# A small conditioning network on TensorE: outputs in four column tiles, transposed back by VectorE

## What is computed

```python
# layer 0, per batch row b; _layer_norm normalizes over the whole 512 x 512 of a row
h = _noise_encoding(t, 128)              # (16, 128), sin and cos
h = silu(h @ W1 + b1)                    # (16, 512)
h = h @ W2 + b2                          # (16, 512)
scale, shift = h @ Wsc + bsc, h @ Wsh + bsh   # (16, 512) each
out = silu(scale * _layer_norm(x, gamma, beta) + shift)
out = out @ W_in + b_in
out = silu(scale * _layer_norm(out, gamma, beta) + shift)
x = out @ W_out + b_out + x
# layer 1, expert e = itok[b]
h = gelu(x @ Wi[e] + bi[e])              # (512, 2048)
r = h @ Wo[e] + bo[e] + x
y = (r - mean) * rsqrt(var + 1e-12) * gamma[e] + beta[e]   # per row of 512
```

## Time and profile before

| | |
|---|---|
| median of three runs | 1784.67 us |
| the profiled execution | 1784.62 us, of which the span of the trace is 1782.8 us |
| TensorE matmuls busy | 1767.7 us, 99% of the span |
| TensorE weight loads busy | 1463.0 us, 82% |
| VectorE busy | 1285.2 us, 72% |
| ScalarE busy | 981.5 us, 55% |
| GpSimd busy | 101.5 us, 6% |
| mean granted TensorE clock | 0.998 of full speed |

### The profile page before, as it was taken

How to read it: one execution, slowest core, us unless ns; L and a number is a source line. 1 busy time by engine, 2 the same in 40 slices (tenths; PEclk the granted TensorE clock), 3 DMA queues, 4 the chain that set the end, 5 groups by cost and what they waited for, 6 DMA issues and landing times.

```text
span 1782.8 us, 22059 instructions
## 1 busy us (share of the span) xinstructions
PE 1767.7 (99%) x7834; PEld 1463.0 (82%) x7834; DVE 1285.2 (72%) x2132; ACT 981.5 (55%) x1562; POOL 101.5 (6%) x197
## 2 busy tenths in 40 slices
PE   9999999999999999999999999999999999999997
PEld 7788888888888888888888888888888888888886
DVE  6956777777677677767777677677777767777565
ACT  6656455565545656456564555555556554565442
POOL 0000000000000000000000000000000000000001
PEclk9999999999999999999999999999999999999999
DMA  7132331423333233332333313333242233322221
GB/s 290 61 124 75 121 110 62 139 101 98 109 100 128 74 118 108 103 110 71 122 109 101 117 61 127 119 107 110 67 142 94 98 110 114 114 74 98 107 95 59
DMA packets 45614, 189.33 MB, mean 106 GB/s; under 512 B 7042, under 2 KB 7042, under 8 KB 29122
## 3 DMA queue, kind: packets, MB, share of 16 engines
q1 hardware_dynamic: 43106, 183.96, 29.2%
q0 software_dynamic: 2400, 3.97, 2.1%
HBM read 171.10 MB, written 16.81 MB: 105 GB/s over the span
## 4 chain that ended last, share of the span: by engine, by line
PE 97%; DVE 1%; issue 0%; DMA 0%; ACT 0%; DVEq 0%; SPq 0%; ACTq 0%
PE out_acc L431 39%; PE hid_ps L431 39%; PE blk_ps L431 18%; DMA x<-in_xT 0%; DVE bn L693 0%; PE blk_ps L375 0%; PE hid_ps L375 0%; PE blk_ps L384 0%; DVE bn_r L812 0%; DVE r_sb L807 0%; ACT work L593 0%; DVE x L761 0%; ACT h_hi L528 0%; DVE x_lo L679 0%; DVE work L748 0%
## 5 line engine op out<-in xcount | busy, mean ns | idle before, releaser
L431 PE MATMUL hid_ps<-x_hi,wi_hi 128*128 128x512 f32 x1024 | 398.7, 389 | 0.5 <-DVE x_lo L679 0.5
L431 PE MATMUL hid_ps<-x_hi,wi_lo 128*128 128x512 f32 x1024 | 398.4, 389 | 0.0
L431 PE MATMUL hid_ps<-x_lo,wi_hi 128*128 128x512 f32 x1024 | 398.4, 389 | 0.0
L431 PE MATMUL out_acc<-wo_hi,g_hi 128*128 128x512 f32 x1024 | 398.3, 389 | 0.0
L431 PE MATMUL out_acc<-wo_lo,g_hi 128*128 128x512 f32 x1024 | 398.3, 389 | 0.0
L431 PE MATMUL out_acc<-wo_hi,g_lo 128*128 128x512 f32 x1024 | 398.3, 389 | 0.0
L581 ACT ACTIVATE g_sb<-hid_ps,bi_sb 128x512 f32<-128x512 f32 x256 | 175.9, 687 | 319.5 <-PE hid_ps L431 319.2
L679 DVE TENSOR_TENSOR g_lo<-g_sb,g_hi 128x512 fp32r<-128x512 f32 x256 | 175.2, 684 | 203.1 <-ACT g_hi L585 201.3
L528 ACT ACTIVATE wo_hi<-stage 128x512 fp32r<-128x512 f32 x256 | 162.0, 633 | 175.9 <-PE out_acc L431 175.9
L679 DVE TENSOR_TENSOR wo_lo<-stage,wo_hi 128x512 fp32r<-128x512 f32 x256 | 176.2, 689 | 71.8 <-ACT wo_hi L528 68.3
L431 PEld LDWEIGHTS hid_ps<-x_hi,wi_hi 128*128 128x128 f32 x1024 | 192.3, 188 | 41.9 <-DVE x_lo L679 1.7
(11 more groups left out here) (91 smaller groups left out, 1664.2 us busy)
## 6 DMA issues: line engine op xcount, KB each, us to landing
stage<-in_expert_w SPq DMA_DIRECT2D x128, 1024.0 KB, 4.8
x<-in_xT SPq DMA_DIRECT2D x15, 1024.0 KB, 7.2
out_y<-r_sb SPq DMA_DIRECT2D x15, 1024.0 KB, 5.2
rows<-in_expert_rows SPq DMA_DIRECT2D x16, 512.0 KB, 6.7
mv_all<-mv_dram POOLq DMA_DIRECT2D x30, 128.0 KB, 4.0
stage<-in_cond_w SPq DMA_DIRECT2D x4, 512.0 KB, 8.7
affine_sb<-in_affine SPq DMA_DIRECT2D x4, 512.0 KB, 11.1
stage<-in_W SPq DMA_DIRECT2D x1, 1024.0 KB, 5.9
```

Of the source, the lines that this page charges most:

```text
L431: last = pe.matmul(dst, w[wp], xs[xp], start=start and i == 0, stop=stop and i == 2)
```

## The change

W2 and the scale/shift weights become the moving operand, the activations the stationary one, 32 columns wide (16 batch rows and 16 zeros). The output has 32 rows of batch then, and each of four groups of output features is written to its own 32 partitions of one bank, so that each matmul uses one column tile of 32 columns. A layer (`layer`) is 16 matmuls of 128 moving columns: 4 chunks of the contraction by 4 column tiles. The host orders the columns of W2, Wsc and Wsh so that a transpose in blocks of 32 x 32 by VectorE brings the features back to the partitions. VectorE does this and adds the bias; ScalarE's evacuations of L544 go. Scale and shift come in two halves of one layer each (chunks 0 and 1, chunks 2 and 3), each with a load of 1024 KB, in place of four parts. The new order of loads is layer 0, half 0, layer 1, half 1, layer 2, layer 3. VectorE's order for the first product is written out anew. Paddings: 7 for 9 and 4 for 5 before the W2 layer, and new ones of 4, 1, 5 and 8.

```diff
-            load_whole(w2_raw, W2, ld_w2)
+            load_turned(w2_raw, W2, ld_w2)
             for c in range(DC):
                 sp.dma_start(x_sb[0][:, c, :], xT[0, c * P:(c + 1) * P, :]).then_inc(ld_first[c], 16)
-            load_cond(0)
             load_layer(0)
-            load_cond(1)
-            load_cond(2)
+            load_turned(cond_raw[0], cond_w[0], ld_cond[0])
             load_layer(1)
-            load_cond(3)
+            load_turned(cond_raw[1], cond_w[1], ld_cond[1])
             load_layer(2)
             load_layer(3)
...
                     if p:
-                        sp.wait_ge(s_mmcond, 2 * p)
+                        sp.wait_ge(s_mmcond, p)
                     else:
-                        sp.wait_ge(s_mm2, 2)
+                        sp.wait_ge(s_mm2, 1)
...
-            def group(bank, n, w, src):
+            def layer(bank, src, w):
                 for c in range(DC):
-                    last = pe.matmul(bank[:, n * WIDE:(n + 1) * WIDE], w[:, c, :], src[:, c, :],
-                                     start=(c == 0), stop=(c == DC - 1))
+                    for j in range(P // BLOCK):
+                        last = pe.matmul(bank[BLOCK * j:BLOCK * (j + 1), 0:P], src[:, c, :], w[:, c, j, :],
+                                         start=(c == 0), stop=(c == DC - 1))
                 return last
...
-            keep_warm(hid_ps[0], 9)
+            keep_warm(hid_ps[0], 7)
...
-            keep_warm(hid_ps[0], 5)
+            keep_warm(hid_ps[0], 4)
             pe.wait_ge(s_pad, 1)
             pe.wait_ge(ld_w2, 16)
             pe.wait_ge(s_m1, DC)
-            for m in range(DC):
-                last = group(blk_ps[1 - m // 2], m % 2, w2_raw[:, :, m * P:(m + 1) * P], m1)
...
+            layer(blk_ps[1], m1, w2_raw).then_inc(s_mm2, 1)
+            keep_warm(blk_ps[0], 4)
+            pe.wait_ge(s_average, 1)
+            pe.wait_ge(s_mv, 1)
+            average_of(0, 0, mv[:, 0, 0:1])
+            keep_warm(blk_ps[0], 1)
             pe.wait_ge(s_sq, 1)
             average_of(0, 1, dev[:, 0, 1:2])
...
+            keep_warm(blk_ps[0], 5)
+
+            def scale_shift(h):
+                pe.wait_ge(ld_cond[h], 16)
+                layer(hid_ps[h], m2, cond_raw[h]).then_inc(s_mmcond, 1)
+
+            pe.wait_ge(s_m2, 1)
+            scale_shift(0)
+            keep_warm(blk_ps[0], 8)
...
             first_block(0, 0, [(m, 0) for m in range(DC)])
-            scale_of(DC - 1)
-            shift_of(DC - 1)
+            scale_shift(1)
             first_block(0, 0, [(m, c) for c in range(1, DC) for m in range(DC)])
...
                 if turn_of(b, which) == 0:
-                    act.wait_ge(s_cond, 2 * (c + 1))
+                    act.wait_ge(s_cond, 2 * (c // (DC // HALVES) + 1))
...
             for c in range(DC):
                 w_hi_part(0, c)
-                scale_shift(c)
                 norm_end(0, 0, [c])
...
+            def cond_out(h):
+                dve.wait_ge(s_mmcond, h + 1)
+                dve.transpose(cond_turned[:, h].rearrange("p k c n -> p (k c n)"), hid_ps[h][:, 0:P]) \
+                   .then_inc(s_condturn, 1)
+                dve.wait_ge(s_condturn, h + 1)
...
+                for k in range(2):
+                    dve.tensor_tensor(cond_sb[:, k, half, :], cond_turned[:, h, k, :, 0:B],
+                                      bias[:, k].unsqueeze(2).to_broadcast([P, DC // HALVES, B]), ALU.add) \
+                       .then_inc(s_cond, 1)
+
+            dve.wait_ge(s_mm2, 1)
+            dve.transpose(m_turned[:, :, :].rearrange("p c n -> p (c n)"), blk_ps[1][:, 0:P]) \
+               .then_inc(s_mturn, 1)
+            dve.wait_ge(s_mturn, 1)
+            dve.tensor_tensor(m2[:, :, :], m_turned[:, :, :],
+                              small_sb[:, B2:B2 + DC].unsqueeze(2).to_broadcast([P, DC, BLOCK]), ALU.add) \
+               .then_inc(s_m2, 1)
             for m in range(DC):
                 stats(0, 0, m)
             first_mean(0)
             centre(0, 0, 0)
             first_var(0)
...
+            affine(0, 0, 0)
+            w_lo_part(0, 0)
+            cond_out(0)
+            centre(0, 0, 1)
+            h_lo_part(0, 0, 0)
+            affine(0, 0, 1)
+            w_lo_part(0, 1)
+            h_lo_part(0, 0, 1)
+            centre(0, 0, 2)
+            affine(0, 0, 2)
+            cond_out(1)
+            w_lo_part(0, 2)
+            centre(0, 0, 3)
+            h_lo_part(0, 0, 2)
+            affine(0, 0, 3)
+            w_lo_part(0, 3)
+            h_lo_part(0, 0, 3)
...
             pool.memset(m1[:, :, B:], 0.0).then_inc(s_pad, 1)
-            pool.memset(m2[:, :, B:], 0.0).then_inc(s_pad, 1)
```

More of the change, by code:

```diff
@@ L158, in build @@
         enc_sin = sb("enc_sin", [P, B])
[L159 to L162, removed]
+        m1 = sb("m1", [P, DC, BLOCK])
+        m2 = sb("m2", [P, DC, BLOCK])
+        m_turned = sb("m_turned", [P, DC, BLOCK])
+        cond_turned = sb("cond_turned", [P, HALVES, 2, DC // HALVES, BLOCK])
+        cond_sb = sb("cond_sb", [P, 2, DC, B])
         bn = sb("bn", [P, DC, 6])
@@ L182, in build @@
         t_sb, cc, small_sb = head_sb[:, 0:B], head_sb[:, B:B + 3], head_sb[:, B + 3:]
-        w2_raw = stage[:, 0].rearrange("p a b n -> p (a b) n")
-        def cond_raw(m):
-            return stage[:, 1 + m // 2, m % 2].rearrange("p k (c n) -> p k c n", n=P)
+        w2_raw, *cond_raw = (stage[:, n].rearrange("p a b (j n) -> p (a b) j n", n=P)
+                             for n in range(1 + HALVES))
         w_raw = [r_sb, x2_turned]
@@ L196, in build @@
         ld_head, ld_idx, ld_w1, ld_w2 = (sem(f"ld_{n}") for n in ("head", "idx", "w1", "w2"))
-        ld_cond = [sem(f"ld_cond{m}") for m in range(DC)]
+        ld_cond = [sem(f"ld_cond{h}") for h in range(HALVES)]
         ld_first = [sem(f"ld_first{c}") for c in range(DC)]
@@ L280, in load_whole, with load_turned @@
                 sp.dma_start(dst[:, :, :], src.rearrange(chunked, p=P)).then_inc(done, 16)
-            def load_cond(m):
-                sp.dma_start(cond_raw(m), cond_w[m].rearrange("p (k c n) -> p k c n", k=2, n=P)) \
-                  .then_inc(ld_cond[m], 16)
+            def load_turned(dst, src, done):
+                sp.dma_start(dst.rearrange("p c j n -> p (c j n)"), src).then_inc(done, 16)
             def load_layer(c):
@@ L541, in _ @@
                                bias=small_sb[:, B1 + m:B1 + m + 1]).then_inc(s_m1, 1)
[L543 to L551, removed]
-                act.wait_ge(s_mmcond, m + 1)
-                cond_part(scale_sb[:, m, :], cond_bank[m], 0, BSC + m).then_inc(s_cond, 1)
-                cond_part(shift_sb[:, m, :], cond_bank[m], 1, BSH + m).then_inc(s_cond, 1)
             def w_hi_part(n, c):
@@ L862, in _ @@
             first_var(0)
-            for c in range(DC):
-                affine(0, 0, c)
-                w_lo_part(0, c)
-                if c + 1 < DC:
-                    centre(0, 0, c + 1)
-                h_lo_part(0, 0, c)
+            affine(0, 0, 0)
[15 more added lines that the diff above has]
+            h_lo_part(0, 0, 3)
             w_lo_part(1, 0)
@@ L1042 @@
                                axis=1),
-        "W1": A["W1"], "W2": A["W2"],
-        "cond_w": np.stack([A["Wsc"], A["Wsh"]]).reshape(2, DC, P, DC, P).transpose(3, 2, 0, 1, 4)
-                    .reshape(DC, P, 2 * DC * P),
+        "W1": A["W1"],
+        "W2": A["W2"].reshape(DC, P, DC, P // BLOCK, BLOCK).transpose(1, 0, 3, 2, 4).reshape(P, DC * D),
+        "cond_w": np.stack([A["Wsc"], A["Wsh"]])
+                    .reshape(2, DC, P, HALVES, DC // HALVES, P // BLOCK, BLOCK)
+                    .transpose(3, 2, 1, 5, 0, 4, 6).reshape(HALVES, P, DC * D),
         "affine": np.stack([A["gamma"].T, A["beta"].T]).reshape(2, DC, P, S).transpose(1, 2, 0, 3)
```

26 lines of the change are left out of this document (6 added, 20 removed).

## The result

The changed kernel takes 1788.59 us in the median of 22 runs (1786.02 to 1789.0), the kernel before 1784.84 us in 22 runs beside it (1784.42 to 1785.94). The ratio is 1.0016, 95% interval 1.001 to 1.0022. So the change is slower, by about as much as the 0.2% that parts "within" from "slower" in the forecast; the forecast itself was slower by 0.7. The time lies in the range. The profiled execution took 1788.71 us, 4.09 more than that of before; its span is 1786.9 us, 4.1 more.

The account below looks back on a forecast made before the run. TensorE, busy throughout from 100 to 1760 us, was taken to bound the kernel, so a shift in the first layer product carries to the end. The steps summed to +0.7 us: 1784.62 + 0.7 = 1785.3 us, range 1783.6 to 1789.3.

Parts of the forecast that it names:

- the mark: Moment TensorE gets past the first layer product (products of chunks 1 to 3 done), 31.89 us before; forecast +0.7 us.
- step 1: W2's layer on TensorE: four column tiles overlap, about 1.0 us per layer, its sum there at about 8.75 us.
- A: Column tiles overlap only by half: 1.9 us per layer, the mark at +2.7, 1787.3 us; chance 0.17.
- B: Column tiles don't overlap: 3.7 to 4.2 us per layer, the mark +8.1 to +9.6, 1792.7 to 1794.2 us; chance 0.10.
- rival D: Loads of W2 and cond_w land earlier in 8 KB rows, W2 by 0.5 to 1 us: 1784.6 us; chance 0.13.
- rival C: TensorE's clock falls while idle before the mean, slowing paddings and half layer: 1786.9 to 1789.3 us; chance 0.15.
- Step 2: VectorE's queue: W2's transpose and addition, 0.45 us, before the statistics, starting at 9.25 for 8.26; first affine +0.6 us.
- Step 3: First silu at 17.05 for 15.85, five paddings hidden; products of chunk 0 at 19.4 for 18.93, +0.45 us left.
- Step 4: Chunks 1 to 3: second half layer saves 0.85 us, shape changes cost 0.3, chunk 2 waits for VectorE; the mark +0.7.

Follow-up runs that it names:

- run 3: Changed kernel with 9 and 5 paddings at the start for 7 and 4, and 12 for 4 after W2's layer: 1784.84 us.
- run 2: Changed kernel with 12 paddings instead of 4 between W2's layer and the first average: 1786.61 us.
- run 4: Changed kernel with VectorE's transpose and addition of W2's sum moved behind the statistics and the small steps of mean and variance: 1784.43 us.
- run 5: Run 3 with the loops of `layer` exchanged, so four matmuls in a row use one column tile: 1790.72 us.
- run 10: Run 9 with 9 and 5 paddings at the start, as in the kernel before: 1785.25 us.
- run 1: Changed kernel with 9 and 5 paddings at the start, as before, instead of 7 and 4: 1789.41 us.
- run 6: Kernel before with 7 and 4 paddings at the start instead of 9 and 5: 1784.88 us.
- run 7: Run 4 with the second half layer amid chunk 0's products, and VectorE's centre(2), affine(2), cond_out(1) before h_lo(1), affine(3) before h_lo(2): 1785.02 us.
- run 9: Run 7 with 8 paddings instead of 4 between W2's layer and the first average: 1785.17 us.
- run 8: Changed kernel without the 4 paddings between W2's layer and the first average: 1788.62 us.
- run 11: Run 4 with 6 paddings for 4, second half layer before chunk 0's products, cond_out(1) before h_lo(1), affine(3) before h_lo(2): 1784.24 us.

## Why the prediction came out as it did

**Where it was right.** That the change is worth its shift of the mark: +4.02 there, +4.1 at the end, the stretch from 100 to 1760 us unchanged. That the column tiles overlap: step 1 took 1.0 us for a layer, and 1.01 us from its start to the next matmul was measured at full clock (a record of 1.08), against half overlap (A) and none (B). That VectorE's queue is where the cost sits. That the loads come earlier, as rival D had it: W2 landed 5.4 us after its issue at 1.66 where it had taken 5.9, the first half at 5.24 + 8.9 = 14.1 for 14.8, the second at 6.75 + 11.9 = 18.7 for 19.3; but in after nothing on the path waited for them. And run 3, the change with its clock held and its rise early, is the case forecast: statistics 9.49 (forecast 9.25), first average 12.40 (12.3), first silu 16.65 (17.05), mark +0.33 (+0.7), 1784.84 us (1785.3).

**The step that failed: the clock.** Steps 1 to 4 were all priced at full pace, and the clock was left to rival C, at 0.15. In after C is the case: idle 2.42 us (C said 2.7), the five paddings 2.48 (2.1), the half layer 1.94 (2.0). Run 2 takes it away for 2.1 us of mark. C had +2.3 in all, of which 0.7 is the forecast itself, so it priced the fall at 1.6. Its path was another in one place: it let the eight paddings hold chunk 0, but they were done at 21.98 and the products at 22.69 waited for `h_lo(0)`. What spoke against C, that the matmuls of the averages lie in between, was wrong: they are four short records behind the idle time, and nothing is in it.

**The step that wasn't there.** The rest, 1.6 us by run 3 against run 2, is the late rise, which no case named. So it is luck in part that the time lies in the range: 3.3 us above the forecast, with 1.6 of the 4.0 us of shift from a cause that the prediction had at nothing. "The layer starts when W2 lands, at 7.65 as now" took one execution of before, with its early rise, as given; in after W2 landed at 7.1 and the layer started at 8.31, behind paddings at half pace, and took 1.89 us. Rows 8 had the sign of it, the nine paddings 0.43 us apart; the question when that ends wasn't asked. Run 4 shows why it matters in this order: the delay enters through the statistics, which the change queued behind the layer. So the 1788.59 us lie within C's 1786.9 to 1789.3 for a reason other than C's own upper end: chunk 0 ran at full clock (records 0.23 us apart from 23.0 on).

**Step 2.** Transpose and addition take 10.27 to 10.83, 0.56 us for 0.45. The statistics came at 10.83 for 9.25: 0.66 by the layer's start, 0.86 by its pace, the rest by VectorE. From the first average to the first affine it took 2.59 us in after and 2.28 in run 3, where step 2 had 2.8: that term was too large by 0.5, which is most of why run 3 lies below the forecast. The sum of step 4 had a slip beside it: it let chunk 3 start "about 28.8" in the kernel before, where TensorE starts it at 29.01 in its timeline, so its own 29.5 makes the mark +0.5 and not +0.7.

**Step 3.** The silu came at 20.34 for 17.05. 1.23 us of it were there at the affine (16.33 for 15.1); the other 2.1 come from TensorE: the silu waited for `cond_out(0)`, and that for the half layer, which the slow paddings held until 17.66. Forecast "hidden", the five paddings were in the path as soon as they ran at half pace.

**Step 4.** The round of chunk 2 goes as forecast: `h_lo(2)` releases it, in after at 29.97, with the same +3.3 as chunk 0 had. The change of shape: from the last product of chunk 0 at 25.31 to the layer at 25.63 it is 0.09 us more than from product to product, from the first product of chunk 1 at 26.64 to the next at 26.98 0.11 more. In the kernel before, where no tile changes, the same two distances are 0.23 (21.54 to 21.77) and 0.31 us (23.47 to 23.78), so only 0.03 of the 0.11 is new. That makes 0.12 for the two, forecast 0.3, ends 0 and 0.3. The Trainium skill, TensorEngine Tiling (Array Packing), Key Properties, says that a change of tiling mode drains TensorE; if these 0.12 us are that drain, it is a small one here.

**Rival B** had its price too high: with the tiles one after another a layer takes 2.39 us (run 5). The 0.115 us between records of 128-wide weights was no bound for 32-wide ones, which follow each other after 2.39 / 32 = 0.075 us.

**What stays open.** What sets the moment of the rise. By the traces it isn't the number of paddings: with 9 and 5 it was early in before and in runs 3 and 10 and late in runs 1 and 5, with 7 and 4 early in runs 6, 7 and 9 and late in after and in runs 2, 4, 8 and 11. And which of two executions of after near 1786.5 us rose early and which didn't fall: only the mean clock (0.996 or 0.998) tells them apart, and one execution of each kernel was traced.

## What to carry to other kernels

Before a step goes ahead of others in an engine's queue, ask not only what it takes but what happens to all behind it if its input comes late; here the same late layer cost 1.6 us ahead of the statistics and nothing behind them. Where a change makes one engine faster in front of a wait, price the stretch behind the wait at both levels of the clock, and if you fill the wait, see how much of it is left: four paddings, with 2.42 us left, were worth nothing, twelve, with 0.61 left, 2 us. Before you blame a clock that fell, see whether the stretch is on the path: in run 7 it wasn't. A padding in front of real work is free only as long as it runs at full pace.

## What the runs showed of the hardware

- TensorE's clock fell from 2.4 to 1.2 GHz after idle times of 3.53 us (run 8), 2.42 (after), 1.64 (run 7) and 0.85 (run 6). It didn't fall after 2.42 in run 1 or after 0.87 in before: the length of the idle time alone didn't decide.
- The rise at the start, as the pace has it, comes before the W2 layer in some executions (five paddings in 1.41 us) and in or after it in others (five in 2.48), in programs that are the same up to there (runs 3 and 1); the column of granted clock says 1.00 in both.
- Four column tiles of 32 columns in turn: 32 records of 128 columns, float32, in 1.01 us at full clock; the same 32 with the four matmuls of each tile in a row: 2.39 us.
- 1024 KB in rows of 8 KB landed 5.4 us after the issue where rows of 2 KB took 5.9. Affine tile 2 landed 12.7 us after its issue in after, 13.8 in run 9, 12.5 in run 4 and 14.2 in run 3, with the same order of loads: an order of VectorE that hangs on such a landing is worth what the later one allows.
